# Conditioning projections from high and low halves, one division for two heads, merge orders drawn anew

## What is computed

```python
query = seq2 + b_self
key = jnp.concatenate([seq1 + b_prev, seq2 + b_self], 1)
value = jnp.concatenate([seq1, seq2], 1)
q = query @ Wq + bq
k = key @ Wk + bk
v = value @ Wv + bv
score_self = (q * k[own row]).sum(-1, keepdims=True) * SCALE
...
attn = jax.nn.softmax(sim, axis=-1)       # the local attention of a layer
out = jnp.einsum('bhwij,bhwjd->bhwid', attn, bv)
x = x + h @ w2 + b2                        # the end of a layer
```

## Time and profile before

| | |
|---|---|
| time, median of 3 runs | 3533.99 us (3531.66 to 3534.14) |
| span of the profiled execution | 3530.7 us; its own time is not given apart, the median lies 3.3 us above the span |
| TensorE busy | 3456.5 us, 98% |
| VectorE busy | 2573.7 us, 73% |
| ScalarE busy | 2312.5 us, 65% |
| GpSimd busy | 742.2 us, 21% |
| mean of the TensorE clock granted | 0.988 of full speed |

### The profile page before, as it was taken

The page is one execution under the profiler, slowest core; times in us unless marked ns, Lnnn a source line. Parts: engine busy times, 40 slices in busy tenths (PEclk is TensorE's granted clock), DMA queues, the critical chain, the costliest instruction groups (busy, mean ns, idle before and its releaser), DMA issues.

```text
span 3530.7 us, 58337 instructions
## 1 busy us (share of the span) xinstructions
PE 3456.5 (98%) x20452; PEld 2423.6 (69%) x20452; DVE 2573.7 (73%) x7101; ACT 2312.5 (65%) x5077; POOL 742.2 (21%) x882
## 2 busy tenths in 40 slices
PE   7899999999999999999999999999999999999997
PEld 4566776767776667777667777667767667767665
DVE  4577777777777777777777777777777777777764
ACT  2466766766766766766766766766666766666764
POOL 2221222121222122222112222112222212222111
PEclk8899999999999999999999999999999999999999
DMA  5210111111111101111101111101111101111000
GB/s 170 34 24 15 19 31 31 31 25 17 21 31 31 31 21 18 25 31 31 31 21 18 25 31 31 31 21 18 25 31 31 31 17 18 29 31 25 7 7 10
DMA packets 99201, 99.56 MB, mean 28 GB/s; under 512 B 9568, under 2 KB 97504, under 8 KB 98912
## 3 DMA queue, kind: packets, MB, share of 16 engines
q1 hardware_dynamic: 97552, 93.36, 15.2%
q10 hardware_dynamic: 1360, 2.47, 0.2%
HBM read 36.02 MB, written 8.39 MB: 13 GB/s over the span
## 4 chain that ended last, share of the span: by engine, by line
PE 88%; DVE 6%; ACT 4%; issue 2%; DMA 0%; POOL 0%; SPq 0%; POOLq 0%; ACTq 0%; DVEq 0%
PE ps L1114 14%; PE ps L1009 12%; PE ps L1125 8%; PE ps L1090 6%; PE ps L1023 6%; PE ps L1080 5%; PE ps L1069 5%; PE ps L1058 4%; PE ps L924 4%; PE ps L914 3%; PE ps L897 3%; PE ps L1043 3%; PE ps L868 3%; ACT attn_area L746 3%; PE ps L860 2%; PE ps L949 2%
## 5 line engine op out<-in xcount | busy, mean ns | idle before, releaser
L625 POOL TENSOR_TENSOR inv<-ssq_f,minus_half 128x16 f32<-128x16 f32 x128 | 419.4, 3276 | 1057.2 <-DVE ssq_f L1320 1057.1
L746 ACT ACTIVATE attn_area<-attn_area,f_nb,inv 128x128 f32<-128x128 f32 (+1 forms) x1024 | 546.1, 536 | 117.4 <-DVE f_nb L1348 116.6
L1114 PE MATMUL ps<-feed_area,w_s 128*128 128x256 f32 x2560 | 606.1, 382 | 4.2 <-DVE feed_area L1383 3.7
L1114 PEld LDWEIGHTS ps<-feed_area,w_s 128*128 128x128 f32 x2560 | 467.4, 190 | 88.0 <-issue 25.4
L1257 DVE TENSOR_REDUCE c_mx<-ps 128x2 f32<-128x512 f32 x512 | 348.7, 687 | 134.5 <-PE ps L897 132.5
L699 ACT ACTIVATE cond_area<-ps 128x512 f32<-128x512 f32 x512 | 298.9, 592 | 62.4 <-PE ps L914 59.1
L1344 DVE CUSTOM_DVE_ANT_0 attn_area<-ps,cst 128x128 f32<-128x128 f32 (+1 forms) x1024 | 303.4, 351 | 43.3 <-issue 41.2
L1394 DVE SCALAR_TENSOR_TENSOR feed_area<-ps,b_s,feed_area 128x256 f32<-128x256 f32 (+1 forms) x448 | 213.7, 477 | 138.8 <-ACT feed_area L772 123.0
L1125 PE MATMUL ps<-feed_area,w_s 128*128 128x256 f32 x1280 | 293.9, 381 | 0.3 <-DVE feed_area L1394 0.3
L1359 DVE TENSOR_SCALAR attn_area<-attn_area,f_inv 128x128 f32<-128x128 f32 (+1 forms) x1024 | 258.0, 315 | 9.1
L470 DVE COPY attn_area<-ps 128x384 f32<-128x384 f32 x256 | 141.8, 554 | 165.5 <-PE ps L1069 165.4
(11 more groups left out here) (144 smaller groups left out, 6516.0 us busy)
## 6 DMA issues: line engine op xcount, KB each, us to landing
cond_area<-cond_area SPq DMA_DIRECT2D x384, 128.0 KB, 4.6
res_rows<-in_x SPq DMA_DIRECT2D x32, 256.0 KB, 2.7
out<-res_rows SPq DMA_DIRECT2D x32, 256.0 KB, 2.1
x_rows<-in_x SPq DMA_DIRECT2D x31, 256.0 KB, 2.7
f_rows<-in_side SPq DMA_DIRECT2D x31, 256.0 KB, 3.0
wqkv_s<-in_wqkv SPq DMA_DIRECT2D x2, 1536.0 KB, 9.7
cond_area<-cond_area SPq DMA_DIRECT2D x128, 6.0 KB
w_s<-in_w SPq DMA_DIRECT2D x2, 768.0 KB, 12.3
```

Source lines behind the costliest of these rows:

```text
L625: nc.gpsimd.tensor_tensor(inv[:, l, t, :], ssq_f[:, l, t, :], minus_half[:, :], ALU.pow).then_inc(SL[l]["inv_norm"], 1)
L746: nc.scalar.activation(soft[:, h % SOFT, lo:hi], soft[:, h % SOFT, lo:hi], ACT.Exp, bias=f_nb[:, l, q, h:h + 1], scale=inv[:, l, q, h:h + ...
L1114: last = mm(ps[:, N0 + f % 2, c * N:(c + 1) * N], w1_s[:, l, k, lo:lo + P], hn[:, k, :], start=(k == 0), stop=(k == KD - 1))
```

## The change

Three things are done. First, the weights of the conditioning projections and the turned inputs are each kept as two tiles of type float32r: a high half, rounded by the copy that writes it, and a low half, what is left of the value. Every product of these projections is made as low x high, high x low and high x high. VectorE makes the low halves of the inputs by two subtractions (after the copies), and those of the weights once, at the start, 512 numbers per partition for each of wk, wq and wv; the bias products through these weights are made in fp32 from both halves, in two calls each. `cw_raw` and `cw_low` share their place, and the tiles of the conditioning area are at a fixed address. Second, `normalize` makes one reciprocal instruction with the sums laid out as (head, tile) and each result written twice, and one multiplication over both heads (2 x 3 x 128 numbers per partition, the factor broadcast along the last 128); `turn_probs` of either head waits for it. Third, all strings of `ORDER`, `HEAD` and `TAIL` are new; the cuts are the same. On TensorE the steps from `rows` to the first projection are now: `rows`, `variance` of the first layer (L1103, two records), the scores of the second layer's first quad (L1058, 16 records), `project` 0. In the first sequence VectorE splits wk before its `rows` step, wq before its `project` 1 and wv before `project` 3. The core of the diff:

```diff
+F32R = mybir.dt.float32r
...
-        "SARARSNRARSRASASSRAANSARSASSNSSNSANSSNARSRSAAASRNSSSAARASNASAAARNNSSANARASARARANRSAARNAASAASRAANSARS"
-        "ASASNRASSSANNRSASSAANAANASRSANANSASSANAARASASASARNAS"),
+        "ASARSRARNRARSANSARSAASSARSSRNASSARSNASRSNSSAAANARAASASSNASSSNANAARSAAANSSAANRAASRRAANRSARAANASASNSSR"
+        "ANSSRSASSANNASANANRSRANRSAAANASSSSASANAARASARSASNAAS"),
...
-    in_turned=2, in_copied_dve=1, in_copied_act=1,
+    in_turned=2, in_high_dve=1, in_high_act=1, in_split=2,
...
-    inv_sum=HP, probs_scaled=FH * 2, p_turned=FH, p_copied_act=len(ACT_TURNS), p_copied_dve=FH - len(ACT_TURNS),
+    inv_sum=HP, probs_scaled=HP, p_turned=FH, p_copied_act=len(ACT_TURNS), p_copied_dve=FH - len(ACT_TURNS),
...
-        cw_s = sb("cw_s", [P, KD, 3 * D])
+        cw_raw, cw_low = (nc.alloc_sbuf_tensor_at(name, [P, KD, 3 * D], dt, offset=COND_AT - 4 * KD * 3 * D)
+                          for name, dt in (("cw_raw", F32), ("cw_low", F32R)))
+        cw_high = sb("cw_high", [P, KD, 3 * D], F32R)
...
-        in_T = front.take(2 * KD * N).rearrange("p (s k t) -> p s k t", s=2, k=KD)
+        in_T, in_low = (nc.alloc_sbuf_tensor_at(name, [P, 2, KD, N], F32R, offset=COND_AT + 4 * front.at
+                                                + 4 * 2 * KD * N * a) for a, name in enumerate(("in_high", "in_low")))
+        front.take(2 * 2 * KD * N)
...
-        f_sum = sb("f_sum", [P, DEPTH, TILES, FH])
-        f_inv = sb("f_inv", [P, DEPTH, TILES, FH])
+        f_sum = sb("f_sum", [P, DEPTH, FH, TILES])
+        f_inv = sb("f_inv", [P, DEPTH, FH, 2 * TILES])
...
+            def products(to, held, moved):
+                for k in range(KD):
+                    for a, b in ((1, 0), (0, 1), (0, 0)):
+                        last = mm(to, held(k, a), moved(k, b), start=(k == 0 and a == 1),
+                                  stop=(k == KD - 1 and a + b == 0))
+                return last
...
+                pe.wait_ge(cw_split, 2)
                 for b in range(KD):
                     for k in range(KD):
-                        last = mm(ps[:, R0, b:b + 1], cw_s[:, k, D + b * P:D + (b + 1) * P],
-                                  cols[:, V_PREV + k:V_PREV + k + 1], start=(k == 0), stop=(k == KD - 1))
+                        for w in (cw_low, cw_high):
+                            last = mm(ps[:, R0, b:b + 1], w[:, k, D + b * P:D + (b + 1) * P].bitcast(F32),
+                                      cols[:, V_PREV + k:V_PREV + k + 1], start=(k == 0 and w is cw_low),
+                                      stop=(k == KD - 1 and w is cw_high))
...
+                pe.wait_ge(cw_split, 4)
                 for k in range(KD):
-                    last = mm(ps[:, T0, :], bwide[:, k, :], cw_s[:, k, 0:2 * D], start=(k == 0), stop=(k == KD - 1))
+                    for w in (cw_low, cw_high):
+                        last = mm(ps[:, T0, :], bwide[:, k, :], w[:, k, 0:2 * D].bitcast(F32), start=(k == 0 and w is cw_low),
+                                  stop=(k == KD - 1 and w is cw_high))
...
-                        pe.wait_ge(S["in_copied_dve"], upto(seq, "in_copied_dve", 1))
-                        pe.wait_ge(S["in_copied_act"], upto(seq, "in_copied_act", 1))
+                        pe.wait_ge(S["in_split"], upto(seq, "in_split", 2))
                         for b in range(KD):
-                            for k in range(KD):
-                                last = mm(ps[:, C0, b * N:(b + 1) * N], cw_s[:, k, D + b * P:D + (b + 1) * P],
-                                          in_T[:, 0, k, :], start=(k == 0), stop=(k == KD - 1))
+                            last = products(ps[:, C0, b * N:(b + 1) * N],
+                                            lambda k, a: (cw_high, cw_low)[a][:, k, D + b * P:D + (b + 1) * P],
+                                            lambda k, a: (in_T, in_low)[a][:, 0, k, :])
                     elif n < 3:
                         t = n - 1
                         if n == 2:
                             pe.wait_ge(S["key_rest"], upto(seq, "key_rest", KD))
-                        for k in range(KD):
-                            last = mm(ps[:, C0 + n % 2, :], in_T[:, 1, k, t * P:(t + 1) * P],
-                                      cw_s[:, k, 0:2 * D], start=(k == 0), stop=(k == KD - 1))
+                        last = products(ps[:, C0 + n % 2, :],
+                                        lambda k, a: (in_T, in_low)[a][:, 1, k, t * P:(t + 1) * P],
+                                        lambda k, a: (cw_high, cw_low)[a][:, k, 0:2 * D])
                     else:
                         s = n - 3
                         if s == 0:
...
                         else:
                             pe.wait_ge(S["query_rest"], upto(seq, "query_rest", 1))
                         for t in range(TILES):
-                            for k in range(KD):
-                                last = mm(ps[:, C0 + s, t * D:(t + 1) * D], in_T[:, s, k, t * P:(t + 1) * P],
-                                          cw_s[:, k, 2 * D:3 * D], start=(k == 0), stop=(k == KD - 1))
+                            last = products(ps[:, C0 + s, t * D:(t + 1) * D],
+                                            lambda k, a: (in_T, in_low)[a][:, s, k, t * P:(t + 1) * P],
+                                            lambda k, a: (cw_high, cw_low)[a][:, k, 2 * D:3 * D])
...
-                    pe.wait_ge(SL[l]["probs_scaled"], upto(seq, "probs_scaled", 2 * h + 2))
+                    pe.wait_ge(SL[l]["probs_scaled"], upto(seq, "probs_scaled", h // 2 + 1))
...
+            def split_weights(n, lo):
+                V.tensor_copy(cw_high[:, :, lo:lo + D], cw_raw[:, :, lo:lo + D]).then_inc(cw_split, 1)
+                dve.wait_ge(cw_split, 2 * n + 1)
+                V.tensor_tensor(cw_low[:, :, lo:lo + D], cw_raw[:, :, lo:lo + D], cw_high[:, :, lo:lo + D].bitcast(F32),
+                                ALU.subtract).then_inc(cw_split, 1)
+            def key_weights():
+                dve.wait_ge(wk_loaded, 16)
+                split_weights(0, D)
...
+                dve.wait_ge(wq_loaded, 16)
+                split_weights(1, 0)
...
+                split_weights(2, 2 * D)
...
-                                  ).then_inc(S["in_copied_dve"], 1)
+                                  ).then_inc(S["in_high_dve"], 1)
+                    for s, high in enumerate(("in_high_dve", "in_high_act")):
+                        dve.wait_ge(S[high], upto(seq, high, 1))
+                        V.tensor_tensor(in_low[:, s], ps[:, C0 + s, :].rearrange("p (k t) -> p k t", k=KD),
+                                        in_T[:, s].bitcast(F32), ALU.subtract).then_inc(S["in_split"], 1)
...
-                    V.reciprocal(f_inv[:, l, :, 2 * p:2 * p + 2], f_sum[:, l, :, 2 * p:2 * p + 2]).then_inc(SL[l]["inv_sum"], 1)
+                    V.reciprocal(f_inv[:, l, 2 * p:2 * p + 2, :].rearrange("p h (q a) -> p h q a", a=2),
+                                 f_sum[:, l, 2 * p:2 * p + 2, :].rearrange("p h (q a) -> p h q a", a=1)
+                                 .broadcast_to([P, 2, TILES, 2])).then_inc(SL[l]["inv_sum"], 1)
                     dve.wait_ge(SL[l]["inv_sum"], upto(seq, "inv_sum", p + 1))
-                    for h in (2 * p, 2 * p + 1):
-                        for q in range(TILES):
-                            lo, hi = (0, P) if q == 0 else (P, 3 * P)
-                            V.tensor_scalar(soft[:, h % SOFT, lo:hi], soft[:, h % SOFT, lo:hi],
-                                            f_inv[:, l, q, h:h + 1], None, ALU.mult).then_inc(SL[l]["probs_scaled"], 1)
+                    both = soft[:, (2 * p) % SOFT:(2 * p) % SOFT + 2, :].rearrange("p h (c k) -> p h c k", c=3)
+                    V.tensor_tensor(both, both, f_inv[:, l, 2 * p:2 * p + 2, 1:4].rearrange("p h (c a) -> p h c a", a=1)
+                                    .broadcast_to([P, 2, 3, P]), ALU.mult).then_inc(SL[l]["probs_scaled"], 1)
...
-            run(dve, "DVE", step, {(0, "part", 1): key_side, (0, "project", 1): masks, (0, "project", 3): values_there,
+            run(dve, "DVE", step, {(0, "rows", 0): key_weights, (0, "part", 1): key_side, (0, "project", 1): masks, (0, "project", 3): values_there,
```

72 lines of the change are left out of this document (38 added, 34 removed).

## The result

The kernel after takes 3504.51 us, median of four runs (3503.72 to 3504.92), against 3532.82 (four runs, 3531.65 to 3534.14) for the kernel before on the same chip: the ratio is 0.9916, with a 95% interval of 0.9903 to 0.993. That is 28 us saved, where 55 were forecast. The profiled execution took 3504.12 us with a span of 3502.3.

A forecast was written before the change was run, and what follows sets the result against it. TensorE's streaming was taken to bound the middle. Profiled span 3530.7 us, less 62.5 for the projections, plus 6 for the start, plus 3.3 around the span, gives 3477.5 us; own range 3457 to 3500, stretched to 3515.

The forecast's parts named there:

- rival (c): TensorE waits at first projection and turned probabilities, up to 1.8 us a sequence: 3534 us, half of that 3505; chance 0.09.
- The likeliest case: In the middle, projections stream in 6.66 us a sequence instead of 8.62, weight loads hidden: 3477 us, chance 0.78.
- (a): At the projections the weight load doesn't hide: 0.22 us per 256-column call, +105 us, 3640 us; chance 0.07.
- (b): At the projections each float32r call streams like an fp32 record, 0.216 and 0.43 us: +138 us, 3678 us; chance 0.06.
- One sign of being wrong: TensorE waits at the first projection or the turned probabilities of over 0.5 us a sequence would refute the forecast.
- The float32r step: At the projections, a 256-column call taken at 0.113 us, 512 columns at 0.216: 1.96 us saved a sequence.
- The bounds of 0.109 and 0.117: At the projections, us per 256-column float32r call with the load hidden: 67 and 58 us saved over 32 sequences.
- The redrawn orders are otherwise worth zero: New instruction orders gain nothing, as the old order leaves TensorE only 3.6 us of waits in 1000 us.
- Part 2: Before the first projection, two VectorE subtractions, 1.36 us a sequence, covered by other TensorE work: zero; uncovered 32 us in all.
- Part 3: At the softmax division, joining saves VectorE about 0.05 us a pair, first head 0.43 us later: taken as zero.
- The upper bound of 110 us: At the softmax division, each of 8 pairs a sequence 0.43 us late: +110 us over the run.
- Part 4: At the start, weight splits, a further subtraction and bias products delay the first sequence 6 us; bounds 3 and 12.

## Why the prediction was right, and where it was not

The range held the time and the direction was right, but the forecast of 3477 us lies 27 too low, and 3504.5 is outside its own range of 3457 to 3500. It is held by the stretch that was added for the nearer half of rival (c), whose half way point was 3505. That it fell there is in part luck: the middle doesn't wait as (c) had it, and half of the shortfall came from a head and a tail that nobody had priced so. The likeliest case's mechanism stands: the middle is bound by TensorE's streaming, float32r calls are one record at about half an fp32 record, the weight load hides. Rivals (a) and (b) are out by the steps of 0.118 and 0.232 us against their 0.22 to 0.43. (Their times were not summed alike: the 3678 us of (b) has the 6 us of the start in it, the 3640 of (a) doesn't.) One sign of being wrong, over 0.5 us a sequence of waiting at the turned probabilities, is absent in the view and present by the steps, 0.62 us; but that place had 0.63 before, so the sign could not tell the two apart.

**The float32r step, "I take 0.113, and 0.216 for 512 columns": sized too small.** Measured 0.118 and 0.232. The bounds of 0.109 and 0.117 went by 256 columns alone and missed both: I had looked for the surplus in the weight load, and at 512 columns nearly all of it stays with 32 weight columns (232 of 234 ns). 1.96 - 1.58 = 0.38 us a pass, 11 us over the body: all of the body's shortfall, since there the next three errors cancel.

**"The redrawn orders are otherwise worth zero": wrong, on both sides.** Alone they are worth 16 us (-18.1 in the body, +3.8 in the tail, and -1.9 in the head, within its spread). I read the 3.6 us in 1000 as all that could be won; at the turned probabilities alone the new orders took out 0.61 us a pass, where that view shows 0.38. And they are the condition of the gain: without them the same instructions take 88 us more. A part that costs 1.4 us of an engine that is idle a quarter of the time needed its place in the order.

**Part 2, "I cost it at nothing": right where I looked, wrong beyond.** The place named, the first projection, has its cover (the wait for one half changed nothing). I asked what the subtractions delay on TensorE's next step, not what they delay on VectorE: 2.23 us a pass under the old orders at three later places and 0.22 of it at the projections, 0.29 under the new. (The subtractions' own price was right: 686 ns by the group above, 680 taken.) That is rival (c)'s amount by another way, and the new orders are why it did not come.

**Part 3, "I take zero": wrong.** VectorE's price was right (0.963 estimated, 960 ns measured), the moment was not: the first head comes about 0.43 us late, and the trace of before already had TensorE waiting there, 0.63 us a pass by the steps, so that slack was short. "Only 10 waits showed" counted those long enough for the view. Joined, it costs 1.0 us a pass under the old orders and 0.33 under the new, 14 us in all (9.7 in the body, 4.2 in the tail, and 0.5 in the head, within its spread). The upper bound of 110 us had it inside; nothing was too low a value to take, since 10 waits at one line say that this line is the next to be late.

**Part 4, the start: 6 us forecast, 13 measured** (the first score from 30.54 to 43.57 us), one over the upper bound. I counted the instructions and not where the function put them in VectorE's order: wq's split stood behind the placed keys, wv's behind the masks. Moving them gives 10.1 of the 13 back at the first score. And the sum had no term for TensorE's clock. From 32.28 us to the first score TensorE doesn't wait, but for most of that time its clock is at half; the 24 calls there take 5.00 us instead of 24 x 0.118 = 2.8, the 44 one-column products 6.3 instead of 44 x 0.114 = 5.0. These 3.5 us (an estimate from these steps) are part of the 13.

**The tail: nothing forecast, 9.1 us lost.** Split by the runs, each part on top of the one before: the new strings +3.8, the halves +1.2, the join +4.2. (The split depends on the order: under the old strings halves and join together leave the tail 0.7 us shorter, 210.4 against 211.1.) With no other sequence to fill in, each wait is bare: TensorE's waits at the turned probabilities in the kernel after, from 3380 us to its end (us in total, times, longest), were

```profile
PE ps L1092 <- DVE attn_area L1400: 7.1, 5, 2.0
```

against 5.3 with the old division. That is 1.8 us of the join's 4.2, and about half of the tail's 9.1 is not waiting at all. The busy time over the tail, of the kernel before and of the kernel after, shows it for the same 977 records of TensorE (engines with counts, TensorE clock, DMA share, GB/s):

```profile
3316.20:3527.30 211.10, 188.26 (x977) 132.82 (x975) 119.39 (x370) 114.77 (x258) 29.03 (x17) 0.97 0.03 8
```

```profile
3278.70:3498.90 220.20, 192.76 (x977) 136.45 (x975) 118.68 (x321) 115.12 (x258) 29.36 (x17) 0.95 0.03 8
```

The records are busy 4.5 us longer at a mean granted clock of 0.95 instead of 0.97; the other 4.6 us are idle time. So a wait here costs its own length and some of the clock behind it.

The three parts, each on top of the one before in the order orders, halves, join, come to -16, -27 and +14 us by the spans, which is the 28 measured. What of the new orders makes them better was not tried string by string, and whether a search made for the old division and the halves would end below 104.62 us a pass stays open.

## What to carry to other kernels

Where an engine is busy over 99% of the middle, cost a change by that engine's streaming first, but cost what it adds elsewhere by what is queued behind it on its own engine, and keep the merge order and the edits apart in the test: here the same edits were worth -28 us with one order and +61 with another. Joining instructions of two consumers saved 0.05 us of 1.0 here, where the engine's time goes by the element, and moves the first consumer to the end of the pair: do it only if nobody waits there. And price the ends of the program by themselves, by where each new instruction stands in its engine's order and with the clock that the waits leave.

## What the hardware showed beyond what was expected

- A float32r call of 512 columns steps at 0.232 us and one of 256 at 0.118, some 7 to 8% over bf16; with the clock at half the same 256-column call steps at 0.213 us, 256/1.2, with no surplus.
- The same subtraction of 512 elements took VectorE 0.69 us at 10.30 us (in the kernel with the splits moved) and 1.52 and 1.53 us at 16.23 and 30.65 (in the kernel after). In the slow cases GpSimd had begun a tensor_tensor of its own 0.29 us earlier; in the fast one it was idle from 9.98 to 15.94 us. The timeline of GpSimd in the kernel after:

```profile
15.94 1.26 POOL L624 TENSOR_TENSOR cond_area<-cond_area 128x512 bf16<-128x512 f32 x1 [5.96 <-DVE cond_area L1279]
30.36 1.27 POOL L624 TENSOR_TENSOR cond_area<-cond_area 128x512 bf16<-128x512 f32 x1 [13.16 <-DVE cond_area L1285]
```

Who begins first decides, and the rest of the same trace shows it. Both slow subtractions end 0.55 us after GpSimd's instruction, and so do 30 of VectorE's multiplications of 512 elements in SBUF (L1375) that began behind a GpSimd tensor_tensor (L643); 0.55 us is about what VectorE needs for 512 elements at its 133 ns per 128. Where VectorE begins first, 0.16 us ahead of the same GpSimd line L624, it keeps its 0.68 us (L1424, 29 times) and GpSimd takes 1.55 us instead of 1.16 to 1.27. An addition that reads PSUM is not held: in the kernel with the splits moved one took 0.69 us at 25.65 (L1268) inside a GpSimd tensor_tensor that began at 25.54. Nor is the subtraction for wk, 0.69 us at 6.32, inside a GpSimd memset from 6.06 to 9.73. So in these rows, where both read SBUF and VectorE has both its operands there, the second to begin waits for the first. A copy can be held too: that of wk, which began at 4.96 inside an earlier memset, took 1.33 us, where those of wq and wv took 0.42.
- Idle time in the view of the waits is short of the true one by up to the 0.16 us that each record is drawn too long: 0.63 us a pass before at the turned probabilities, where it shows 0.38.
